# Quantised attention: one PSUM bank per half of the heads for probabilities times values

## The chip, the cores and the metric

The kernel runs on one core of a Trainium2 chip. The time is the device time of one execution in microseconds (us); lower is better. The core has a matrix engine (TensorE, PE in the rows, its weight loads PEld), a vector engine (VectorE, DVE), a scalar engine (ScalarE, ACT), a general engine (GpSimd, POOL) and a queue engine that issues transfers (SyncE, SP). Each engine works through its own instructions in order, and engines wait for each other on semaphores.

## What is computed

A transformer block on 16 sequences of 256 tokens, 512 channels, followed by a second, unquantised attention. The change concerns the two quantised attentions of the first block, 16 heads of 32 channels each. Cut to what matters:

```python
q, k, v = (x @ wq), (ctx @ wk), (ctx @ wv)             # split into 16 heads of 32
sim  = einsum('bhid,bhjd->bhij', fq(q), fq(k)) * SCALE  # fq: rounding to 8 bits
attn = softmax(sim, axis=-1)
out  = einsum('bhij,bhjd->bhid', fq(attn), fq(v))       # <- the products of the change
x    = out @ wo + bo + x
```

It runs twice for each sequence: first on the sequence itself, then with `ctx` as the source of keys and values. Then come a layer norm, a gated feed-forward part and the last attention.

## The kernel before

The program has three stages one after another: the quantised attentions of all 16 sequences (to about 1,275 us), and two halves of the feed-forward part, the second of which holds the last attention. The change touches only the first.

The first stage is a chain of 32 **phases**. A phase is one attention of one sequence; `Phase.a` is 0 for the first attention, 1 for the second. A loop of 13 rounds (`ROUNDS`) runs one phase of the second attention (`two_`) and one of the first attention (`one_`) per round, a 14th round is written out behind it, and two phases stand ahead of the loop and two behind (`P_Y`, `P_Z`). A phase has eight **steps** g = 0 to 7, one for each group of two heads. The order in every step is written by hand, the same for each round:

- TensorE (`pe_phase`): the scores of group g+1 into the PSUM tile `S` (line 495, four matmuls), then transposes if the step has any (line 137), then `pe_pv`, the products of probabilities and values of group g-3 into the tile `O` (line 516, four matmuls), then the step's **fill**, one half of a projection into a PSUM tile `PJ` (lines 162 and 153, 3 to 3.7 us each). In steps 0, 1 and 2 `pe_pv` still serves groups 5, 6 and 7 of the phase before.
- ScalarE (`act_phase`): `act_shift`, which reads the last fill out of `PJ` (line 556); in two steps `act_oT` (line 595); then `act_exp`, four exponentials of group g out of `S` into `e` (line 586), each with a read of its row sums.
- VectorE (`dve_phase`): the row maxima of group g+1 (line 675), then the transposed layer norm if any (lines 191, 663, 670), then `dve_probs` of group g-1, which scales, rounds and clips the probabilities to `pq` (lines 683, 692, 700) around the rounding of the projections (lines 635, 645), and in some steps layer-norm statistics and `xhat` (lines 112, 117, 129) or residuals (line 720).
- SyncE (`turn_probs`): the transfer that transposes `pq` to `pT` (line 869), from which `pe_pv` reads.

`O` is one PSUM bank: 128 partitions by 2 x 256 values, room for eight heads, which is half of the 16. So it is used twice in a phase: groups 0 to 3 (half 0) and groups 4 to 7 (half 1). `act_oT` copies a finished half into `oT` and counts `oT_done`; ScalarE does this for half 0 in step 7 of the phase and for half 1 in step 3 of the next phase, both times behind `act_shift` and ahead of `act_exp`. The first products of a half, groups 0 (TensorE's step 3) and 4 (TensorE's step 7), wait until the other half has been copied:

```python
if g % (GROUPS // 2) == 0 and not (isinstance(ph.n, int) and ph.n == 0 and g == 0):
    pe.wait_ge(oT_done, 2 * ph.n + g // (GROUPS // 2))
```

Two more waits of TensorE matter here. `pe_scores` of group g+1 waits until all four exponentials of group g-1 have read the same `S` buffer (`exp_done`). The transposes of the layer norm wait for `xhat` from VectorE. In PSUM, `S` takes four banks, `O` one, `PJ` two.

Of the kernel before, what the change touches and what calls it, by code (L numbers as in the profile page):

```python
# [5 lines left out]
P = 128  # L6
ALU = mybir.AluOpType
ACT = mybir.ActivationFunctionType
# [6 lines left out]
B, TOK, D = 16, 256, 512  # L15
TT = TOK // P
KC = D // P
H0, DH0 = 16, 32
# [3 lines left out]
GROUPS = H0 // 2  # L22
# [14 lines left out]
def build(nc, t, out):  # L37
# [3 lines left out]
    def sb(stack, name, shape, dt=F32):  # L41
        return stack.enter_context(nc.sbuf_tensor(name, shape, dt))

    def ps(stack, name, shape, dt=F32):
        return stack.enter_context(nc.psum_tensor(name, shape, dt))

    def sem(name):
        return ctx.enter_context(nc.semaphore(name))

    with ctx:  # L50
# [287 lines left out]
        with ExitStack() as one:  # L338
# [13 lines left out]
            oT = sb(one, "oT", [P, KC, TOK])  # L352
# [16 lines left out]
            delta_w4 = sb(one, "delta_w4", [P, 2, 4])  # L369

            S = [ps(one, f"S{i}", [P, 2, 2, TOK]) for i in range(2)]
            O = ps(one, "O", [P, 2, TOK])
            PJ = [ps(one, f"PJ{i}", [P, 512]) for i in range(2)]

            ln = ln_sems("ln")
# [26 lines left out]
            oT_done = sem("oT_done")  # L402
# [21 lines left out]
            def wait_filled(eng, where):  # L424
                eng.wait_ge(pj_filled[bank_of(where[0], *where[2:])], before(*where) + 1)
# [74 lines left out]
            def turned_count(ph, g, groups_back=0):  # L500

                n = GROUPS // 2 * ph.n + g // 2 + 1 - groups_back // 2
                return 16 * n

            def pe_pv(pe, ph, g):
                pe.wait_ge(probs_turned[g % 2], turned_count(ph, g))
                if g == 0:
                    pe.wait_ge(quantised, ph.v_at)
                if g % (GROUPS // 2) == 0 and not (isinstance(ph.n, int) and ph.n == 0 and g == 0):

                    pe.wait_ge(oT_done, 2 * ph.n + g // (GROUPS // 2))
                for i in range(2):
                    h = 2 * g + i
                    r = DH0 * (h % 4)
                    for kc in range(TT):
                        ins = nc.tensor.matmul(O[r:r + DH0, (h // 4) % 2, :],  # L516
                                               vQ[ph.a][:, kc, h * DH0:(h + 1) * DH0],
                                               pT[:, g % 2, 4 * i + kc:4 * i + kc + 3:2, :], start=(kc == 0),
                                               stop=(kc == TT - 1))
                ins.then_inc(pv_done, 1)  # L520

            def pe_phase(pe, ph, prev, nxt):
                for g in range(GROUPS):
                    if g + 1 < GROUPS:
                        pe_scores(pe, ph, g + 1)
                    elif nxt:
                        pe_scores(pe, nxt, 0)
                    fills = ph.steps(g)
                    for name, j in fills:
                        if kind_of(name) in ("hT", "h2T", "ctxT"):  # L530
                            pe_fill(pe, at(ph.stage, ph.b, name, j))
                    if g >= 3:
                        pe_pv(pe, ph, g - 3)
                    elif prev:
                        pe_pv(pe, prev, g + GROUPS - 3)
                    for name, j in fills:
                        if kind_of(name) not in ("hT", "h2T", "ctxT"):
                            pe_fill(pe, at(ph.stage, ph.b, name, j))

            def pe_drain(pe, ph):  # L540

                for g in range(3):
                    pe_pv(pe, ph, g + GROUPS - 3)
# [46 lines left out]
            def act_oT(act, ph, half):  # L590
                act.wait_ge(pv_done, ph.group((half + 1) * GROUPS // 2))
                if half == 0 and ph.o_fill:

                    wait_filled(act, ph.o_fill)
                nc.scalar.activation(oT[:, 2 * half:2 * half + 2, :], O[:], ACT.Copy,  # L595
                                     scale=wv_scale[:, ph.a:ph.a + 1]).then_inc(oT_done, 1)

            def late(ph, prev, g):
# [10 lines left out]
            def act_phase(act, ph, prev):  # L609
                for g in range(GROUPS):  # L610
                    if ph is P_A:
                        for c in chunks_beside(g):
                            act_weight_high(act, c)
                    for where in late(ph, prev, g):
                        if kind_of(where[2]) in QUANTISED:
                            act_shift(act, where)
                    if g == 7:
                        act_oT(act, ph, 0)
                    if g == 3 and prev:
                        act_oT(act, prev, 1)  # L620
                    for where in transposed(ph, g, 0):
                        act_transposed(act, where)
                    act_exp(act, ph, g)

            def act_drain(act, ph):
                for where in late(None, ph, 0):
                    act_shift(act, where)
                act_oT(act, ph, 1)
# [1136 lines left out]
```

## Time and profile before

| | us |
|---|---|
| median of 3 runs | 3103.09 (3102.81 to 3108.14) |
| the profiled execution | 3102.73, of which the span of the trace is 3100.9 |
| TensorE busy | 2824.2 (91% of the span) |
| VectorE busy | 1766.5 (57%) |
| ScalarE busy | 1444.9 (47%) |
| GpSimd busy | 680.3 (22%) |

The shares are means over stages with different limits. In the feed-forward stages TensorE is busy 97% and more of the time; in the first stage, TensorE and VectorE are both near 90%. The largest idle time of TensorE in the page's groups that belongs to the changed line is 99.7 us ahead of line 516, of which 51.6 us ended with the copy of line 595.

### The profile page before, as it was taken

How to read it: one execution, taken by the hardware profiler on the slowest of the kernel's cores; microseconds unless marked ns; L12 is line 12 of the kernel's file. 1: busy time of each engine (PE TensorE's matmuls, PEld its weight loads, DVE VectorE, ACT ScalarE, POOL GpSimd, SP SyncE). 2: the span in 40 equal slices, each digit the busy share in tenths (PEclk: the TensorE clock that was granted, in tenths of full speed). 3: DMA queues.
4: the chain of work that ended last, by engine and by line, in shares of the span. 5: the costliest groups of instructions: out<-in, count | busy, mean ns of one | idle time of the engine just before them, and what ended most of it. 6: DMA issues, size and time to landing. Idle time of an engine off the chain costs nothing. (4 is left out here: it accounts for less than half of the span.)

```text
span 3100.9 us, 54841 instructions
## 1 busy us (share of the span) xinstructions
PE 2824.2 (91%) x18304; PEld 2272.1 (73%) x18304; DVE 1766.5 (57%) x4468; ACT 1444.9 (47%) x3747; POOL 680.3 (22%) x1147
## 2 busy tenths in 40 slices
PE   3689999999899897499999997999999999999997
PEld 2456666666666664299999996888888888888886
DVE  4689898888989886543333334334433444334432
ACT  3477777776777774321111112444444444444442
POOL 0122222222222221133333332111111111111110
PEclk8899999999999998699999998999999999999997
DMA  5243343333333332320000004000000000000000
GB/s 150 45 72 78 78 88 78 81 77 79 85 78 80 86 73 57 97 101 27 27 27 27 27 34 129 25 30 27 27 34 27 27 27 27 27 27 27 34 14 14
DMA packets 328217, 168.59 MB, mean 54 GB/s; under 512 B 276960, under 2 KB 293344, under 8 KB 328160
## 3 DMA queue, kind: packets, MB, share of 16 engines
q1 hardware_dynamic: 328160, 167.87, 21.2%
q8 instruction: 31, 0.51, 0.1%
q14 instruction: 26, 0.21, 0.0%
HBM read 75.54 MB, written 25.17 MB: 32 GB/s over the span
## 5 line engine op out<-in xcount | busy, mean ns | idle before, releaser
L586 ACT ACTIVATE e<-S,bias,qk_scale 128x256 f32<-128x256 f32 x1024 | 563.1, 563 | 67.1 <-DVE e L692 62.9
L675 DVE TENSOR_REDUCE negmax<-S 128x4 f32<-128x1024 f32 x256 | 312.0, 1220 | 98.3 <-PE S L495 96.6
L692 DVE TENSOR_SCALAR e<-e,rsum 128x256 f16<-128x256 f32 x1024 | 291.2, 347 | 2.9
L556 ACT ACTIVATE shifted<-PJ,round_col,inv 128x512 f32<-128x512 f32 x192 | 149.1, 777 | 259.0 <-PE PJ L162 259.0
L153 PE MATMUL PJ<-w_a_wo,oT 128*128 128x512 f32 x512 | 243.2, 620 | 2.6 <-ACT oT L595 1.8
L1561 POOL TENSOR_TENSOR mid_partsB<-mid_actB,mid_partsB 128x256 fp32r<-128x256 f32 x128 | 101.1, 790 | 638.6 <-DVE mid_partsB L1466 638.6
L162 PE MATMUL PJ<-hT,w_a_wq 128*128 128x256 f32 x1536 | 203.4, 290 | 22.9 <-DVE w_a_wq L416 19.3
L162 PEld LDWEIGHTS PJ<-hT,w_a_wq 128*128 128x128 f32 x1536 | 191.2, 195 | 35.7 <-issue 35.7
L586 ACT ACTIVATION_READ_ACCUMULATOR e<-S,bias,qk_scale 128x1 f32 x1024 | 208.4, 203 | 0.0
L162 PE MATMUL AG0B<-h_partsB,upB 128*128 128x256 f32 x1536 | 199.8, 287 | 7.1 <-POOL h_partsB L1556 6.0
L162 PE MATMUL AG0A<-h_partsA,upA 128*128 128x256 f32 x1536 | 199.6, 287 | 7.1 <-POOL h_partsA L1556 3.4
L162 PEld LDWEIGHTS AG0A<-h_partsA,upA 128*128 128x128 f32 x1536 | 191.6, 194 | 15.5 <-issue 9.8
L162 PE MATMUL AG1A<-h_partsA,upA 128*128 128x256 f32 x1536 | 196.8, 285 | 5.4 <-DVE downA L1413 5.4
L162 PEld LDWEIGHTS AG0B<-h_partsB,upB 128*128 128x128 f32 x1536 | 193.1, 192 | 11.1 <-issue 7.6
L162 PEld LDWEIGHTS AG1A<-h_partsA,upA 128*128 128x128 f32 x1536 | 194.1, 194 | 9.6 <-issue 5.8
L162 PE MATMUL AG1B<-h_partsB,upB 128*128 128x256 f32 x1536 | 199.6, 286 | 0.0
L516 PE MATMUL O<-pT,vQ 128*32 128x256 bf16 x1024 | 107.0, 289 | 99.7 <-ACT oT L595 51.6
L162 PEld LDWEIGHTS AG1B<-h_partsB,upB 128*128 128x128 f32 x1536 | 188.2, 191 | 5.2 <-issue 5.0
L1459 DVE SCALAR_TENSOR_TENSOR mid_actB<-AG1B,c_ff_b,gateB 128x256 f32<-128x256 f32 x64 | 31.0, 484 | 270.3 <-ACT gateB L1367 270.3
L1561 POOL TENSOR_TENSOR mid_partsA<-mid_actA,mid_partsA 128x256 fp32r<-128x256 f32 x128 | 100.4, 784 | 385.5 <-DVE mid_partsA L1466 385.5
L769 POOL TENSOR_TENSOR bias<-negmax,qk_scale 128x4 f32<-128x4 f32 x256 | 74.4, 291 | 497.5 <-DVE negmax L675 495.5
L153 PEld LDWEIGHTS PJ<-w_a_wo,oT 128*128 128x128 f32 x512 | 95.1, 195 | 114.1 <-issue 111.2
(180 smaller groups left out, 5570.0 us busy)
## 6 DMA issues: line engine op xcount, KB each, us to landing
x_in<-in_x_dram SPq DMA_DIRECT2D x16, 512.0 KB, 3.7
ctx_in<-in_ctx_dram SPq DMA_DIRECT2D x16, 512.0 KB, 3.6
mid_dram<-x SPq DMA_DIRECT2D x16, 512.0 KB, 2.7
y_inA<-mid_dram SPq DMA_DIRECT2D x16, 512.0 KB, 3.5
part_dram<-x3A SPq DMA_DIRECT2D x16, 512.0 KB, 3.6
y_inB<-mid_dram SPq DMA_DIRECT2D x16, 512.0 KB, 3.2
kv_in<-in_ctx_dram SPq DMA_DIRECT2D x16, 512.0 KB, 4.6
baseB<-part_dram SPq DMA_DIRECT2D x16, 512.0 KB, 3.2
```

What stands on the lines that cost most here:

```text
L153: last = nc.tensor.matmul(bank[:], xT[:, k, j * P:(j + 1) * P], w[:, k, :], start=(k == 0), stop=(k == KC - 1))
L162: last = nc.tensor.matmul(acc, lhs(l), rhs(r), start=(start and i == 0), stop=(stop and i == 2))
L516: ins = nc.tensor.matmul(O[r:r + DH0, (h // 4) % 2, :], vQ[ph.a][:, kc, h * DH0:(h + 1) * DH0], pT[:, g % 2, 4 * i + kc:4 * i + kc + 3:2, ...
L556: nc.scalar.activation(shifted[:, bank, :], PJ[bank][:], ACT.Identity, bias=round_col[:, 0:1], scale=inv[:, d:d + 1]).then_inc(pj_emptied[ ...
L586: nc.scalar.activation(e[:, s, i, :], S[s][:, i // 2, i % 2, :], ACT.Exp, bias=bias[:, s, i:i + 1], scale=qk_scale[:, ph.a:ph.a + 1], accu ...
L675: nc.vector.tensor_reduce(negmax[:, g % 2, :], S[g % 2][:].rearrange("p i q n -> p (i q) n"), AX_X, ALU.max, negate=True).then_inc(max_don ...
L692: nc.vector.tensor_scalar(e16[:, s, i, :], e[:, s, i, :], rsum[:, s, i:i + 1], ROUND16, ALU.mult, ALU.add).then_inc(prob_scaled, 1)
L769: nc.gpsimd.tensor_tensor(bias[:, g % 2, :], negmax[:, g % 2, :], qk_scale4[:, ph.a, :], ALU.mult).then_inc(bias_done, 1)
L1459: nc.vector.scalar_tensor_tensor(out=mid_act[:, f % 2, :], in0=AG[f % 2][:, 0:TOK], scalar=ff_b1[:, c:c + 1], in1=gate[:, f % 2, :], op0=A ...
L1561: nc.gpsimd.tensor_tensor(mid_parts[:, f % 2, 1, :], mid_act[:, f % 2, :], mid_parts[:, f % 2, 0, :], ALU.subtract).then_inc(mid_low_done, 1)
```

## The change

`O` becomes two PSUM tiles of one bank each, and half h of the heads has its own. The first products of a half then wait for the last copy out of their own bank, which is one copy earlier in the count of `oT_done`: group 0 waits for half 0 of the phase before, group 4 for half 1 of the phase before. The very first phase has no such wait. `act_oT` reads the bank of its half. ScalarE's copies stay where they were, and the order of the matmuls, activations, VectorE operations and transfers is the same on every engine.

```diff
-            O = ps(one, "O", [P, 2, TOK])
+            O = [ps(one, f"O{i}", [P, 2, TOK]) for i in range(2)]
@@ pe_pv
-                if g % (GROUPS // 2) == 0 and not (isinstance(ph.n, int) and ph.n == 0 and g == 0):
-                    pe.wait_ge(oT_done, 2 * ph.n + g // (GROUPS // 2))
+                half = g // (GROUPS // 2)
+                if g % (GROUPS // 2) == 0 and not (isinstance(ph.n, int) and ph.n == 0):
+                    pe.wait_ge(oT_done, 2 * ph.n + half - 1)
@@
-                        ins = nc.tensor.matmul(O[r:r + DH0, (h // 4) % 2, :],
+                        ins = nc.tensor.matmul(O[half][r:r + DH0, (h // 4) % 2, :],
@@ act_oT
-                nc.scalar.activation(oT[:, 2 * half:2 * half + 2, :], O[:], ACT.Copy,
+                nc.scalar.activation(oT[:, 2 * half:2 * half + 2, :], O[half][:], ACT.Copy,
                                      scale=wv_scale[:, ph.a:ph.a + 1]).then_inc(oT_done, 1)
```

## Rows read from the trace of the kernel before

**Rows 1.** Engines by stretch: busy us, TensorE clock, DMA share, GB/s.
```profile
176.00:1181.00 1005.00, 908.76 (x5905) 614.47 (x5904) 894.84 (x2307) 721.44 (x2133) 245.90 (x574) 1.00 0.38 80
```
**Rows 2.** What TensorE waited for: us in total, times, longest.
```profile
PE O L516 <- ACT oT L595: 51.6, 43, 1.2
...
PE PJ L137 <- DVE xhat L129: 22.7, 16, 8.1
```
**Rows 3.** TensorE in time: start, us, line, what, [idle before <-releaser].
```profile
613.14 0.39 PE L495 MATMUL S<-kT,qT 32*128 32x256 bf16 x4
614.74 0.40 PE L516 MATMUL O<-pT,vQ 128*32 128x256 bf16 x4 [1.20 <-ACT oT L595]
...
618.14 0.39 PE L495 MATMUL S<-kT,qT 32*128 32x256 bf16 x4
...
633.18 0.40 PE L516 MATMUL O<-pT,vQ 128*32 128x256 bf16 x4 [1.20 <-ACT oT L595]
...
636.46 0.39 PE L495 MATMUL S<-kT,qT 32*128 32x256 bf16 x4
637.74 1.09 PE L137 MATMUL PJ<-ident,xhat 128*128 128x128 f32 x8 [0.89 <-DVE xhat L129]
...
650.30 0.39 PE L495 MATMUL S<-kT,qT 32*128 32x256 bf16 x4
651.90 0.40 PE L516 MATMUL O<-pT,vQ 128*32 128x256 bf16 x4 [1.20 <-ACT oT L595]
...
655.30 0.39 PE L495 MATMUL S<-kT,qT 32*128 32x256 bf16 x4
...
686.48 0.40 PE L516 MATMUL O<-pT,vQ 128*32 128x256 bf16 x4 [1.20 <-ACT oT L595]
```
**Rows 4.** ScalarE in time: the copy, and the last sum of group 3's exponentials.
```profile
614.00 0.68 ACT L595 ACTIVATE oT<-O,wv_scale 128x512 f32<-128x512 f32 x1
...
616.65 0.22 ACT L586 ACTIVATION_READ_ACCUMULATOR e<-S,bias,qk_scale 128x1 f32 x1
...
653.81 0.22 ACT L586 ACTIVATION_READ_ACCUMULATOR e<-S,bias,qk_scale 128x1 f32 x1
```
**Rows 5.** End of the first stage, in time: how soon a waiter starts.
```profile
1177.30 0.22 ACT L586 ACTIVATION_READ_ACCUMULATOR e<-S,bias,qk_scale 128x1 f32 x1
...
1177.66 0.40 PE L495 MATMUL S<-kT,qT 32*128 32x256 bf16 x4 [2.49 <-ACT e L586]
1177.68 0.42 DVE L700 TENSOR_SCALAR pq<-e 128x1024 bf16<-128x1024 f16 x1
...
1181.36 0.61 PE L516 MATMUL O<-pT,vQ 128*32 128x256 bf16 x4 [0.65 <-DMA pT<-pq]
```
**Rows 6.** VectorE in time.
```profile
618.58 1.23 DVE L675 TENSOR_REDUCE negmax<-S 128x4 f32<-128x1024 f32 x1 [1.76 <-PE S L495]
...
628.43 1.22 DVE L675 TENSOR_REDUCE negmax<-S 128x4 f32<-128x1024 f32 x1 [0.64 <-PE S L495]
...
646.49 0.43 DVE L700 TENSOR_SCALAR pq<-e 128x1024 bf16<-128x1024 f16 x1
...
655.74 1.22 DVE L675 TENSOR_REDUCE negmax<-S 128x4 f32<-128x1024 f32 x1 [0.28 <-PE S L495]
...
660.02 1.23 DVE L675 TENSOR_REDUCE negmax<-S 128x4 f32<-128x1024 f32 x1 [1.08 <-PE S L495]
```
**Rows 7.** Engines in one stretch: busy us of PE, PEld, DVE, ACT, POOL.
```profile
628.43:637.69 9.26, 7.22 (x40) 4.70 (x36) 9.04 (x25) 4.85 (x13) 2.07 (x6) 1.00 0.48 113
```
**Rows 8.** TensorE in time, early and late, where its clock changes.
```profile
29.33 8.32 PE L162 MATMUL PJ<-hT,w_a_wq 128*128 128x256 f32 x48 [19.25 <-DVE w_a_wq L416]
38.12 6.02 PE L162 MATMUL PJ<-hT,w_a_wk 128*128 128x256 f32 x48 [0.47 <-ACT shifted L556]
...
1180.10 0.61 PE L495 MATMUL S<-kT,qT 32*128 32x256 bf16 x4 [1.57 <-ACT e L586]
```

## The prediction

> **What bounds the kernel now.** I read the table of stretches first. Of the three stages the change can only touch the first, so I look at its steady part, 176 to 1181 us, which is 14 equal rounds. There TensorE is busy 908.8 of 1005.0 us and VectorE 894.8 [rows 1]: two engines at 90% and 89%. That warns the reader: time taken from TensorE's idle only counts until VectorE or ScalarE is late instead. The list of waits comes next. TensorE stood still 51.6 us, in 43 waits of 1.2 us, because `O` had not been copied out [rows 2]. The timeline of one round then tells where: in step 3 of the second attention's phase (call it **P1**, 614.74 us), in step 7 of that phase (**P2**, 633.18) and in step 3 of the first attention's phase (**P3**, 651.90), each with 1.20 us [rows 3]. The next P1 is at 686.48, so a round takes 71.74 us. Three places in 14 rounds make 42 waits; the 43rd (**P4**) comes once, in step 7 of the last first-attention phase, where that round's transposes are missing. In the other rounds, step 7 of the first attention has no such wait, since its transposes are themselves late.
>
> Why 1.2 us: ScalarE cannot copy before it has read the last fill out of `PJ`, and this fill ends just as TensorE reaches the products. At P1 the copy runs from 614.00 to 614.68 [rows 4] and the products start at 614.74.
>
> **What the change removes.** With a second bank, the products of group 0 wait for a copy made four steps earlier, those of group 4 likewise; in the hand-written order both are long done. So the wait itself goes at all 43 places. At P3 the next condition is `pT`: `pq` of group 0 ends at 646.49 + 0.43 = 646.92 [rows 6], and a waiting product started 1181.36 - (1177.68 + 0.42) = 3.26 us after the end of its `pq` [rows 5], so `pT` is there at 650.18, ahead of 651.90 - 1.20 = 650.70. The transfer hides, with 0.5 us to spare. The question is what is late next, place by place.
>
> *P1.* The fill starts 1.20 us earlier, and so would the next scores, at 618.14 - 1.20 = 616.94. But they need the exponentials of group 3, which ScalarE still makes behind the copy: the last ends at 616.65 + 0.22 = 616.87 [rows 4]. Waiting scores started 1177.66 - (1177.30 + 0.22) = 0.14 us after such an end [rows 5]; with 0.15 they start at 617.02. Gain 618.14 - 617.02 = **1.12 us**. VectorE idled 1.76 us before its maxima at 618.58, waiting for just these scores [rows 6], so it follows by the full 1.12. Up to step 7 TensorE then leads (VectorE idled again, 0.64 us, before 628.43, released by scores [rows 6]), so the gain is carried on.
>
> *P2.* The next scores would start at 636.46 - 1.20 = 635.26 instead of 636.46. Behind them stand the transposes, and these already wait 0.89 us for `xhat` [rows 3]. VectorE makes `xhat` at the end of a run that begins with the maxima at 628.43 and in which it is busy 9.04 of 9.26 us, up to 637.69 [rows 7]. That run does not start from anything behind P2, so it ends no earlier. TensorE arrives earlier and waits longer, about 2 us in one piece. Gain **0**.
>
> *P3.* As P1: last exponential of group 3 at 653.81 + 0.22 = 654.03 [rows 4], scores at 654.18 instead of 655.30 [rows 3], **1.12 us**. VectorE is tighter here. It idled 0.28 us before the maxima at 655.74, and 1.08 before the next at 660.02 [rows 6]. Together it can take up 1.36 us, more than 1.12, by the second of them; the first moves by only 0.28, but no engine that leads waits for it. The margin is 0.24 us.
>
> *P4.* Same pattern as P1 (copy, exponentials, scores), no transposes behind it; I take 1.1 us.
>
> What the change adds: a bank that nothing else used, at no time. It adds no instruction and no wait, and moves no transfer; the matmuls write the same shapes. TensorE even drops a register operation in two places. I put both at 0. Nothing is queued anew behind a waiting instruction.
>
> **Sum.** 14 x 1.12 (P1) + 14 x 0 (P2) + 14 x 1.12 (P3) + 1.1 (P4) = 32.5 us. The round shrinks from 71.74 to 69.50 us. Against the profiled execution of 3102.73 us this gives **3070.2 us**; that execution lies 0.4 us under the median of 3103.09, so nothing is corrected. Bounds of the size: if scores were bound by TensorE alone, 29 x 1.20 = 34.8 us (3068); if VectorE's 0.24 us at P3 and a similar bit at P1 were used up and 0.9 us stayed of each, 29 x 0.9 = 26 us (3077).
>
> **Rivals.**
>
> *Half.* VectorE, 89% busy, holds the gain at one of P1 and P3; P3 is the likelier with its 0.24 us. Against it speak the two idle times of VectorE there, both released by scores. 3102.7 - 14 x 1.12 - 1.1 = 3085.9 us.
>
> *Moved.* The stall turns into another everywhere, as at P2, because VectorE or the exponentials set the whole round, or because the new count still waits for the same copy. 3102.7 less at most 1.1: 3102. Against it: VectorE's waits for scores of 1.76 and 1.08 us could not be there. The Trainium skill (TensorE: Matmul & The Clock Gate, HAM oscillation) reports a matmul kernel in which PSUM double-buffering gave no further gain. By that the sum would be 0; the trace agrees at P2 and not at P1 or P3.
>
> *Full.* VectorE's run to `xhat` gives way too, so P2 pays as P1 does: 3070.2 - 14 x 1.12 = 3054.5 us. It would need slack inside 9.04 busy of 9.26 us.
>
> *Slower, by the clock.* TensorE now has its longest idle of the round in one piece: 635.3 plus 0.4 for the scores, to 637.74, 2.0 us where it was 1.20 and 0.89 with a fill between. If its clock fell to the lower level there once a round, the work behind would run slowly. The one fill of this shape that began after idling shows the price: 48 matmuls took 8.32 us against 6.02 for the next 48 [rows 8], 2.30 us, and the transposes and products ahead would add up to 1.3 (their own 1.09 + 0.40 doubled, at most 1.5, with some hidden). 14 x 3.6 = 50.4, less 32.5, is 18 us slower: 3121. It decides from 2.24 us a round. For it: near 1180 us four score matmuls took 0.61 instead of 0.39 us [rows 8]. Against it: that came after several idle pieces of 1.6 to 2.5 us in a row, and the scores right behind the 2.49 us piece still took 0.40 [rows 5]. The round's mean clock is 1.00 [rows 1] and the rest of it gets denser. The same page (A second HAM failure mode) tells of a kernel that cycled through PSUM banks and lost to a clock that went down and up between bursts; no row of the loop shows that.
>
> **How the numbers follow.** Forecast (P1 and P3 pay, P2 does not) 0.70; half 0.11; moved 0.07; full 0.05; slower 0.05; the rest, 0.02, between them. The range must reach from the forecast's own bounds to the half case: 3063 to 3087, which holds nearly all of the forecast and the half case, 0.8. What a measurement of this kernel can tell from no change is 0.2%, 6.2 us. Faster by more: forecast, half, full and some of the rest, 0.87. Within: moved, 0.07. Slower: the clock and a bit, 0.06.
>
> **What would show it.** No wait of TensorE on the copy at line 595 in the loop. One P1 every 69.5 us. Scores behind P1 and P3 held 0.1 us by exponentials. The wait for `xhat` grown from 0.9 to about 2 us, with VectorE's run before it as long as now. VectorE's idle before the maxima of step 5: from 1.76 to 0.6 us at P1, from 0.28 to 0 at P3. The clock 1.00 throughout. The forecast is wrong if a round takes more than 70.5 us, if the `xhat` wait stays at 0.9 with a shorter round (full), or if 24-matmul fills behind `xhat` take well over 3.1 us (clock).

## The result, and the profile after

| | us |
|---|---|
| before, median of 4 runs | 3104.09 (3102.81 to 3108.14) |
| changed, median of 4 runs | 3081.43 (3078.53 to 3083.62) |
| ratio | 0.992, 95% interval 0.9906 to 0.9934 |
| profiled execution of the changed kernel | 3083.62, span 3081.8 |

The change gains 22.7 us. The forecast was 32.5 us (3070.2), the range 3063 to 3087. The direction and the range hold; about a third of the gain is missing. The profile tells where.

First the list of what TensorE waited for (us in total, times, longest):

```profile
PE O L517 <- DMA pT<-pq: 49.5, 26, 13.4
PE S L495 <- ACT e L587: 38.7, 17, 5.5
PE PJ L137 <- DVE xhat L129: 38.1, 16, 8.0
```

The 43 waits on the copy, 51.6 us in [rows 2], are gone. The wait for `xhat` has grown from 22.7 to 38.1 us over the same 16 times: 14 rounds in which it is 1.98 us instead of about 0.87. The waits on `pT` and on the exponentials are little changed (47.3 and 39.1 us before).

Now one round of the changed kernel on TensorE, P1 first (start, us, line, what, idle before), and ScalarE's last row sum of that step:

```profile
746.80 0.39 PE L495 MATMUL S<-kT,qT 32*128 32x256 bf16 x4
747.12 0.40 PE L517 MATMUL O<-pT,vQ 128*32 128x256 bf16 x4
...
750.31 0.22 ACT L587 ACTIVATION_READ_ACCUMULATOR e<-S,bias,qk_scale 128x1 f32 x1
...
750.59 0.39 PE L495 MATMUL S<-kT,qT 32*128 32x256 bf16 x4
750.91 1.28 PE L137 MATMUL PJ<-ident,ctx_in 128*128 128x128 f32 x8
```

The products follow the scores at once, and the next scores stand 3.79 us behind the last ones, where it was 618.14 - 613.14 = 5.00 [rows 3]. They start 0.06 us after the exponentials end (750.31 + 0.22 = 750.53). So the scores behind P1 come 1.21 us earlier, where 1.12 was forecast. The transposes behind them take 1.28 us here.

Next the same place, the transposes that wait for `xhat` and the work behind them, in three rounds, near 770, 558 and 979 us:

```profile
770.13 1.09 PE L137 MATMUL PJ<-ident,xhat 128*128 128x128 f32 x8 [1.98 <-DVE xhat L129]
771.15 0.40 PE L517 MATMUL O<-pT,vQ 128*32 128x256 bf16 x4
772.06 3.12 PE L162 MATMUL PJ<-ctxT,w_a_wk 128*128 128x256 f32 x24 [0.51 <-ACT turned L184]
```
```profile
558.19 1.97 PE L137 MATMUL PJ<-ident,xhat 128*128 128x128 f32 x8 [1.98 <-DVE xhat L129]
560.09 0.62 PE L517 MATMUL O<-pT,vQ 128*32 128x256 bf16 x4
560.64 4.89 PE L162 MATMUL PJ<-ctxT,w_a_wk 128*128 128x256 f32 x24
```
```profile
979.16 1.09 PE L137 MATMUL PJ<-ident,xhat 128*128 128x128 f32 x8 [1.98 <-DVE xhat L129]
980.18 0.40 PE L517 MATMUL O<-pT,vQ 128*32 128x256 bf16 x4
981.09 4.61 PE L162 MATMUL PJ<-ctxT,w_a_wk 128*128 128x256 f32 x24 [0.51 <-ACT turned L184]
```

The same instructions take 1.09, 0.40 and 3.12 us in the first, 1.97, 0.62 and 4.89 in the second. In the third only the fill is slow, 4.61 us. The table of stretches has the granted clock (the third number from the end) for the 8 us behind the waits at 558 and 770 us, for the steady part, and for the transposes and for the fill of the third round:

```profile
558.19:566.19 8.00, 8.00 (x45) 6.70 (x45) 6.01 (x14) 4.38 (x12) 2.89 (x4) 0.60 0.17 33
770.13:778.13 8.00, 7.49 (x63) 6.49 (x64) 7.80 (x18) 6.67 (x20) 3.26 (x5) 1.00 0.27 52
176.00:1150.00 974.00, 918.35 (x5870) 627.22 (x5869) 883.50 (x2278) 714.17 (x2106) 251.17 (x568) 0.98 0.39 81
979.16:981.09 1.93, 1.42 (x13) 0.98 (x13) 1.88 (x3) 1.12 (x3) 1.43 (x2) 1.00 0.70 136
981.09:984.50 3.41, 3.41 (x16) 3.41 (x17) 3.27 (x10) 2.72 (x9) 0.20 (x1) 0.50 0.00 0
```

0.60 is a mixture of the two levels: part of the 8 us at 1.2 GHz, the rest at 2.4. In the third round the clock is at the upper level behind the wait and at the lower one (0.50) only in the fill. In the kernel before, the steady part had 1.00 [rows 1]. A busy share of 8.00 of 8.00 us is no good sign here: TensorE is busy because it is slow, and did 45 matmuls where the other round did 63.

How long rounds are can be read from the transposes of `ctx_in`, one set a round:

```profile
538.97 1.28 PE L137 MATMUL PJ<-ident,ctx_in 128*128 128x128 f32 x8
...
610.39 1.29 PE L137 MATMUL PJ<-ident,ctx_in 128*128 128x128 f32 x8
...
750.91 1.28 PE L137 MATMUL PJ<-ident,ctx_in 128*128 128x128 f32 x8
...
820.14 1.28 PE L137 MATMUL PJ<-ident,ctx_in 128*128 128x128 f32 x8
```

A round with the full clock takes 69.23 us, less than the forecast 69.50; one with a fallen clock between 70.1 and 71.42. The clock fell at this wait in 10 of the 14 rounds: in 4 before the transposes started, in 6 behind them. From 188.13 to 1101.94 us, 13 rounds take 913.8 us; 13 rounds of 69.24 would be 900.1. The clock cost 13.7 us there, in 9 slow rounds; the tenth fall lies in the last round, behind 1101.94, and cost about 1.3 us more (65.02 us to the next set, 63.75 in the run e1 below, where the clock did not fall in that round).

### The profile page after: what moved, and what is told of

It is laid out like the page before. It is cut to its first block and busy times, and to the rows that moved or that the text cites. A ratio compares the mean times of both kernels' runs of the same rounds, so it can differ in the third digit from the quotient of the medians.

```text
span 3081.8 us, 54840 instructions
## 1 busy us (share of the span) xinstructions
PE 2841.1 (92%) x18304; PEld 2288.1 (74%) x18304; DVE 1764.8 (57%) x4468; ACT 1447.2 (47%) x3747; POOL 688.3 (22%) x1147
## 5 line engine op out<-in xcount | busy, mean ns | idle before, releaser
L1368 ACT ACTIVATE gateA<-AG0A,c_ff_b 128x256 f32<-128x256 f32 x64 | 30.4, 475 | 270.7 <-PE AG0A L162 270.7
```

## The experiments

**Clock theory**: P1 and P3 pay, P2 only turns two idle pieces (1.20 and 0.89 us with a fill of 3 us between) into one of 1.98 us, and there the clock falls. **Rivals**: P2 is neutral and the falls come from the denser schedule of P1 and P3; or VectorE held the gain at one of the two places.

### One place at a time

The edit chooses which first products still wait for the other half's copy (`a` is 0 for the first attention, 1 for the second):

```diff
-                    pe.wait_ge(oT_done, 2 * ph.n + half - 1)
+                    held = (ph.a, half) in ((1, 1),)      # e1: P2 held
+                    pe.wait_ge(oT_done, 2 * ph.n + half - (0 if held else 1))
```

For e2 the set is `((1, 0), (0, 0), (0, 1))`, for e6 `((1, 1), (0, 0), (0, 1))`, for e7 `((1, 1), (1, 0), (0, 1))`.

**All but P2:**

> Two banks as in the change, but step 7 of the second attention's phase (P2) waits for the other half's copy as before. Theory (the longer idle time before the transposes let TensorE's clock fall): TensorE idles 1.20 us at P2 and about 0.9 us for xhat again, the clock is 1.00 in every round, every round takes 69.2 us as the change's undisturbed rounds did, and the time is that of the change less about 14 us: 3067 us (3064 to 3071). Rival (the lost 11 us is not of P2's making: the new schedule of P1 and P3 itself costs it, or the clock falls because the rounds are denser): the clock still falls in about 10 of 14 rounds and the time stays at 3081.

Measured 3076.2 us (3073.6 to 3080.0), ratio 0.9911 (0.9897 to 0.9924). In its profile, which is of the fastest of the five runs, three of 13 rounds take 70.7 to 70.9 us and the others 69.3 to 69.6; the clock fell at three places in place of ten. One is the wait for `xhat` behind P2; two are in step 7 of the first attention, at the transposes of the other layer norm, where TensorE idles 0.72 us before and 0.76 us behind them, as in the kernel before. So giving back the "gain" at P2 is worth about 5 us. But neither theory's number is met: the falls do not vanish.

**Only P2:**

> Two banks, and only P2 is freed; P1, P3 and P4 wait for the other half's copy as before. Clock theory: P2 gives nothing, since xhat comes no earlier, and the idle time of 2.0 us in one piece makes the clock fall in most rounds at 1.4 to 2.2 us each, so this part alone is slower than the kernel before: 3112 to 3124 us. Rival (freeing P2 is neutral, the clock falls only with P1 and P3 freed): 3103 us, clock 1.00. Rival (P2 pays too): 3088 us.

Measured 3123.9 us (3117.1 to 3125.2), ratio 1.0056 (1.0042 to 1.0069): one part of the change, alone, makes the kernel 19 us slower, as the clock theory said. One of its rounds, TensorE in time: first the wait for `xhat`, then the other layer norm's step. Below them the stretch 176 to 1181:

```profile
572.48 0.40 PE L495 MATMUL S<-kT,qT 32*128 32x256 bf16 x4
574.82 1.97 PE L137 MATMUL PJ<-ident,xhat 128*128 128x128 f32 x8 [1.94 <-DVE xhat L129]
576.71 0.62 PE L518 MATMUL O<-pT,vQ 128*32 128x256 bf16 x4
577.26 3.47 PE L162 MATMUL PJ<-ctxT,w_a_wk 128*128 128x256 f32 x24
...
606.53 1.09 PE L137 MATMUL PJ<-ident,xhat 128*128 128x128 f32 x8 [0.72 <-ACT shifted L558]
607.55 0.40 PE L518 MATMUL O<-pT,vQ 128*32 128x256 bf16 x4
608.71 4.61 PE L162 MATMUL PJ<-w_a_wv,ctxT 128*128 128x512 f32 x12 [0.76 <-DVE turned L191]
```
```profile
176.00:1181.00 1005.00, 921.37 (x5836) 628.81 (x5834) 877.41 (x2259) 706.43 (x2082) 241.84 (x563) 0.97 0.37 78
```

Its rounds take 72.6 and 74.2 us in turn, where the kernel before has 71.74. In every one the clock falls at the wait for `xhat`, which costs 0.9 us here. In the longer ones it falls a second time, in the other layer norm's step, which costs 1.6 us more: the slow fill above, 4.61 us where it takes 3.0. Idle time there is the same as in the kernel before, where no fall happened, so nearly half of what e2 loses in the loop comes from falls at a place that the edit did not touch. The falls happen with P1 and P3 held as before, so the denser schedule is not needed for them.

**Only P1, and only P3:**

> Two banks, only P1 freed; P2, P3 and P4 wait for the other half's copy as before. Theory: 1.2 to 1.3 us a round from P1 alone, 14 x 1.28 = 18 us, unless the clock falls in a few rounds, which P2's wait should mostly prevent: 3086 to 3092 us. Rival (VectorE holds the gain at one of the two places, and the other gave all): 3104 or 3070 us.

Measured 3089.8 us (3087.6 to 3095.3), ratio 0.9958 (0.9945 to 0.9972).

> Two banks, only P3 freed; P1, P2 and P4 wait as before. Theory: 14 x 1.2 = 17 us, 3087 to 3093 us, so that P1 alone and P3 alone add up to both. Rival (VectorE's margin of 0.24 us at P3 was too small and P3 gives little): 3100 us or more.

Measured 3091.2 us (3088.1 to 3092.1), ratio 0.9953 (0.9939 to 0.9966). The rounds are cleaner than the medians, since in each profile the clock still fell twice, once in the other layer norm's step and once at a later wait for `xhat` (0.85 us). P2 is held in both, so freeing P1 or P3 alone also brings a few falls that the kernel before did not have. `ctx_in` transposes of e6, then of e7, from rounds without a fall:

```profile
327.35 1.29 PE L137 MATMUL PJ<-ident,ctx_in 128*128 128x128 f32 x8
...
397.82 1.29 PE L137 MATMUL PJ<-ident,ctx_in 128*128 128x128 f32 x8
```
```profile
687.01 1.35 PE L137 MATMUL PJ<-ident,ctx_in 128*128 128x128 f32 x8
...
757.54 1.35 PE L137 MATMUL PJ<-ident,ctx_in 128*128 128x128 f32 x8
```

70.47 and 70.53 us: P1 gives 1.27, P3 1.21, together 2.48 of the 2.50 that the change's clean rounds gained over 71.74. They add up, and VectorE holds neither. The 0.06 us that P1 has more than P3 are seen in the transposes behind it, which take 1.29 us in e6 and 1.35 in e7.

### Work in the idle time

**Weak work:**

> The change, with the scores of group 1 in the first attention's phases computed four times over (12 more matmuls of 0.08 us, the same output), so that TensorE works about 1.0 us of the 2.0 us in which it waits for xhat. The maxima behind them are not due before. Clock theory: the added 14 x 1.0 us of work costs nothing and keeps the clock up: rounds of 69.2 us, 3067 us. Rival (the clock has nothing to do with the idle time, or added work is added time): 3081 us, or up to 14 us more, 3095.

```diff
-                for i in range(2):
+                again = 3 if ph.a == 0 and g == 1 and ph.stage != "first" else 0
+                for i in [0, 1] * (1 + again):
```

Measured 3077.7 us (3076.8 to 3081.0), ratio 0.9915 (0.9902 to 0.9929). The idle time before the transposes is 1.33 us, and the clock still fell behind it in 8 of 14 rounds. Rounds without a fall take 69.25 us, so the added work cost nothing; but it prevented few falls, and neither expected time was met.

**Full work:**

> The change, with idle matmul work put in front of the layer norm's transposes: seven matmuls of 128x512 (about 0.25 us each) in step 0 of the first attention's phase, two in its step 7, written to the O bank that is free there and overwritten later; the output is the same. Clock theory: TensorE is busy where it waited 2.0 and 0.7 us, the clock never falls in the loop, all rounds take 69.2 us, 3068 us (3065 to 3071). Rival (weak work does it and not idle time, or the falls have another cause such as the denser rounds): rounds with slow k2 fills stay, 3076 to 3090 us.

```diff
+            def keep_busy(pe, ph, prev, g, fills, n0, n7):
...
+                    n, bank = n0, 0                       # here: 7 matmuls, step 0
+                    pe.wait_ge(oT_done, 2 * ph.n - 1)
...
+                    n, bank = n7, 1                       # here: 2 matmuls, step 7
+                    pe.wait_ge(oT_done, 2 * ph.n)
...
+                for i in range(n):
+                    nc.tensor.matmul(O[bank][:].rearrange("p c n -> p (c n)"), wv[:, 0, i % KC, 0:P],
+                                     wv[:, 0, i % KC, :], start=True, stop=True)
...
+                    keep_busy(pe, ph, prev, g, fills, 7, 2)
```

Measured **3068.0 us** (3067.2 to 3069.2), ratio 0.9881 (0.9866 to 0.9896): 13.4 us faster than the change, by adding about 2.6 us of useless matmuls to every round (1.88 us in step 0, 0.73 in step 7). TensorE in one of its rounds:

```profile
619.45 0.40 PE L495 MATMUL S<-kT,qT 32*128 32x256 bf16 x4
619.77 1.88 PE L535 MATMUL O<-w_a_wv 128*128 128x512 f32 x7
621.83 1.09 PE L137 MATMUL PJ<-ident,xhat 128*128 128x128 f32 x8 [0.18 <-DVE xhat L129]
622.86 0.40 PE L517 MATMUL O<-pT,vQ 128*32 128x256 bf16 x4
623.77 3.13 PE L162 MATMUL PJ<-ctxT,w_a_wk 128*128 128x256 f32 x24 [0.51 <-ACT turned L184]
```

The transposes start at the same point of the round as in the change, and what follows them never slows down in the loop: the 13 rounds behind the first set of transposes take 69.24 to 69.44 us, all of them. The 13 rounds take 900.6 us, 13.2 less than the 913.8 of the change, which is nearly all of the 13.7 us that the clock cost there, and about the difference of the medians.

**Less of it:**

> The change with three matmuls of 128x512 in place of seven in front of the transposes of step 0, and two in step 7. About 1.2 us of idle time stay before the transposes, nearly as much as in the run with repeated scores (1.33 us), where the clock fell in 8 of 14 rounds. If the idle time alone decides, falls in several rounds and 3072 to 3078 us. If the kind of work in it decides too (full matmuls against the small score matmuls), no or few falls, 3067 to 3070 us.

Measured 3073.0 us (3068.2 to 3075.8), ratio 0.9904 (0.9889 to 0.9919). In the profile:

```profile
622.02 1.09 PE L137 MATMUL PJ<-ident,xhat 128*128 128x128 f32 x8 [1.09 <-DVE xhat L129]
```

The idle time is 1.09 us, and the clock fell in one round of 14. This profile is of the fastest of the four runs; the two slowest have a lower mean clock (0.963 against 0.965), so they probably had more falls. The median lies in the range expected if idle time alone decides, the profile nearer to the other case, so the run does not separate idle time from the kind of work.

**Control:**

> Control: all waits as in the kernel before (each half's first products wait for the other half's copy), with three and two matmuls of idle work as above. The clock was 1.00 in the kernel before, so there is nothing to win: 3102 to 3106 us. If the idle work gained time by itself and not by the clock, 3095 us or less.

All waits as before, with the three and two matmuls of e9 (not the seven of e5): 3107.7 us (3102.2 to 3110.8), ratio 1.0010 (1.0001 to 1.0019). Idle work was worth nothing here, where the clock did not fall in the loop; a round even takes 71.83 us in place of 71.74.

### Another order

**Products ahead of the transposes:**

> The change, with the products of step 0 and step 7 ahead of the layer norm's transposes instead of behind them. The projection behind them waits for ScalarE's or VectorE's affine step either way, so the order alone gives 0. It takes 0.33 us out of the idle time before the transposes: 1.65 instead of 1.98 us in one piece, and adds it behind them. Clock theory: fewer rounds with a fallen clock than the change's 10 of 14, 3067 to 3078 us. Rival (the clock does not go by this idle time): 3081 us.

```diff
+                    def turns():       # the transposes of the step
...
+                    pv_first = any(kind_of(n) in ("hT", "h2T") for n, _ in fills)
+                    if not pv_first:
+                        turns()
                     if g >= 3:
                         pe_pv(pe, ph, g - 3)
                     elif prev:
                         pe_pv(pe, prev, g + GROUPS - 3)
+                    if pv_first:
+                        turns()
```

Measured 3084.3 us (3078.2 to 3086.2), ratio 0.9928 (0.9914 to 0.9941), no different from the change. The idle time went from 1.98 to 1.65 us in the profile, and the fill behind was slow in 9 of 14 rounds, with one more slow fill at the other layer norm. A miss for the clock theory in this form: 0.33 us less in front of the transposes did not help. The 0.33 us went behind them (0.84 us of idle time there in place of 0.51), so the idle time in front and behind together stayed the same. That this is the reason is a guess; no run tests it.

**xhat ahead of the maxima:**

> The change, with VectorE's row maxima of the next phase's group 0 behind xhat instead of ahead of it. xhat is then ready about 1.1 us earlier and TensorE's idle time before the transposes falls from 2.0 to about 0.9 us. VectorE has the same work and is the one that leads from step 6 to step 2, so no time comes from its order. Clock theory: the clock falls in few rounds, 3068 to 3076 us. Rival (the clock does not go by this idle time): 3081 us. Rival (xhat was the bound of the round): 14 x 1.1 us less, 3055 to 3066 us.

```diff
+                    late_max = g == 7 and nxt and ("o1", 1) in ph.steps(5)
                     if g + 1 < GROUPS:
                         dve_max(dve, ph, g + 1)
-                    elif nxt:
+                    elif nxt and not late_max:
                         dve_max(dve, nxt, 0)
...
                             ln_xhat(dve, ln, x1, xhat, ln_x1(ph.b + 1))
+                    if late_max:
+                        dve_max(dve, nxt, 0)
```

Measured **3067.8 us** (3066.8 to 3068.6), ratio 0.9882 (0.9866 to 0.9897), with no added work. VectorE and TensorE in one round:

```profile
621.40 1.00 DVE L129 TENSOR_SCALAR xhat<-x,mv,rstd 128x512 f32<-128x512 f32 x2
622.32 2.35 DVE L676 TENSOR_REDUCE negmax<-S 128x4 f32<-128x1024 f32 x2
```
```profile
622.46 1.09 PE L137 MATMUL PJ<-ident,xhat 128*128 128x128 f32 x8 [0.85 <-DVE xhat L129]
...
624.39 3.12 PE L162 MATMUL PJ<-ctxT,w_a_wk 128*128 128x256 f32 x24 [0.51 <-ACT turned L184]
```

The two sets of maxima now stand together behind `xhat`; the idle time is 0.85 us, and no fill of the loop is slow. The rounds take 69.1 us, so the order gives only 0.1 us a round of its own, as expected of a stretch that VectorE leads; the rest is the clock. This is the cleanest test: no work is added and every wait on `O` is free.

**Both together:**

> Both mends together: the change, xhat ahead of the next phase's maxima on VectorE, and three and two matmuls of idle work. If xhat ahead of the maxima alone already keeps the clock up in every run, nothing more: 3066 to 3069 us. If some runs of it still lost a round or two, 1 to 2 us less than 3067.8.

Measured 3068.5 us (3068.2 to 3071.2), ratio 0.9886 (0.9871 to 0.9901): nothing on top. Its profiled execution took 3071.2 us without a fall in the loop, so such a spread does not come from the falls alone. The order on VectorE alone suffices.

## Why the prediction came out as it did

- **The waits go at all 43 places**: right, none is left. `pT` stayed hidden at P3.
- **P1 and P3**: the mechanism is right, the size 10% small. Forecast 1.12 each, measured 1.27 and 1.21 (e6, e7). The term that was off is the 0.15 us between the last exponential and the scores, read from the end of the stage; in the loop it is 0.06 (750.53 to 750.59 above). That makes 1.21; the rest at P1 is the shorter set of transposes behind it. VectorE took up the gain at P3 with its small margin.
- **P2**: right that it gives nothing by the order and that `xhat` bounds it. The wait became 1.98 us, forecast "about 2".
- **P4**: forecast 1.1. The scores before it and the scores after it start 4.89 us apart in e7, where P4 is held, and 3.79 us in e1, where it is free. So 1.10 us.
- **The sum**: with the measured terms, 14 x 1.27 + 14 x 1.21 + 1.10 = 35.8 us, or 3066.9 us. e5, in which the clock stays up in the loop, has 3068.0. Less the 15 us that the falls cost in the change, the sum gives about 3082; measured were 3081.4.
- **The clock**: this is the step that failed. The forecast put the price of the longer idle piece at P2 at nothing ("The clock 1.00 throughout"); it cost about 15 us. The rival "slower, by the clock" had the right place and the right cause, and got 0.05. It was taken as all or nothing and argued away by a row: scores right behind a 2.49 us idle piece still ran at full speed [rows 5]. That row says nothing of what comes later. In the same trace of the kernel before, the clock is 1.00 during these scores and 0.51 right after them:

```profile
1177.66:1178.06 0.40, 0.40 (x6) 0.19 (x8) 0.40 (x2) 0.40 (x1) 0.40 (x1) 1.00 0.00 0
1178.06:1181.00 2.94, 1.08 (x8) 0.21 (x8) 2.87 (x9) 2.22 (x9) 0.64 (x3) 0.51 0.47 89
```

  In the change, too, the transposes and products right behind the idle piece were still fast in 6 of the 10 rounds, and only the fill, which begins 1.9 us behind it, was slow. The second argument, that the round's mean clock was 1.00 and the rest gets denser, looked at the round and not at the place that got sparser. By the Trainium skill (TensorE: Matmul & The Clock Gate, A second HAM failure mode), a kernel that cycles through PSUM banks can idle between groups so often that the clock oscillates; the trace agrees so far that the clock goes down and up again, 10 times in 14 rounds, but here the idle piece ends with `xhat` and not with a bank. The price was too high as well: a fall costs 0.9 to 2.2 us of a round, not 3.6, and it came in 10 of 14 rounds. So about 15 us were lost and not 50, and the sign of the sum stayed.
- **The range**: that 3081.4 lies in it is luck in part. Its upper end was set by the half case, in which VectorE holds one of two places; e6 and e7 show that this did not happen. The loss that filled the range is the clock's, which was priced outside it. Of the prediction's own signs of being wrong, slow fills behind `xhat` (4.4 to 4.9 us) are there, and seven of 13 rounds took more than 70.5 us.

Why the clock falls in one round and not in the next is not settled. The falls come in patterns that differ from run to run (mostly every second round in e3, all in e2). Idle time in front of the transposes orders the runs roughly: 1.98 us 10 falls there in the change and 14 in e2, 1.65 us 9, 1.33 us 8, 1.09 us 1, about 0.87 us with P2 held (e1, e6, e7) 1 each, 0.85 us (e8) and 0.18 us none. But the kernel before has 0.84 to 0.94 us and none, and e1, e2, e4, e6 and e7 have 2, 6, 1, 1 and 1 more in the other layer norm's step, whose idle time only e4 changed. So the length of the idle piece is a cause, but not the only thing that decides. The profile is one execution each. In e1 the mean granted clock goes from 0.964 in the fastest run to 0.961 in the slowest, which suggests that the number of falls varies; but the kernel before spreads as well (3100.1 to 3110.7 us, 0.967 to 0.964), though the clock did not fall in its profiled loop.

## What to carry to other kernels

A freed wait pays only as far as the next thing that the engine waits for is ready earlier too; go through the places one by one, as 43 equal waits here were worth 1.27, 1.21, 1.1 and nothing. Where the freed engine only reaches its next wait sooner, freeing it is not neutral: short idle pieces with work between them become one long one, and on TensorE that can cost more than it gave. Here three mends helped: keeping the useless wait (e1, 5 us), filling the gap (e5, 13.4 us), and best, with no added work, bringing forward what is waited for (e8, two VectorE steps swapped, 13.6 us). And a fast instruction right behind an idle piece does not show that the piece is harmless: look a few microseconds further.

## What the runs showed of the hardware

- TensorE's clock fell at a single idle piece of 1.98 us in a loop in which TensorE is over 90% busy, in 10 of 14 rounds. In 6 of the 10 it fell late, 1.5 to 2.3 us behind the piece. In these ten rounds the fill of 24 matmuls of 128x256 takes 4.4 to 4.9 us instead of 3.1 (3.5 in two in which the transposes ahead of it had already run slowly).
- Two idle pieces of 1.20 and 0.89 us with a fill of 3 us between them brought no fall in the kernel before; one of 1.93 to 1.99 us at the same place brought one in every round of e2.
- Full matmuls may keep the clock up better than small score matmuls (32 rows): 1.09 us of idle time with full work had 1 fall of 14, 1.33 us with small work 8. The idle times differ too, and the first count is from the fastest of its runs, so this is a hint and not shown.
- 1.88 us of useless matmuls in a gap of 2.0 us, with 0.73 us in a second gap, in each of 14 rounds, made the kernel 13.4 us faster.
